# A two-layer Mamba, attention and expert kernel: one ring of PSUM banks for the B and C rows, the causal mask moved to VectorE, GpSimd's norm work placed behind the scans, and the output stage rearranged

## The reference, cut to what matters

```python
xn = layernorm(x)
# layer 0, branch s: Mamba, then an MLP
x_, z = split(xn @ in_proj.T);  x_ = silu(causal_conv(x_))
dt, Bm, Cm = split(x_ @ x_proj.T)            # 8, 16 and 16 numbers a row
dt = softplus(dt @ dt_proj.T + bias)
h[t] = exp(dt * A) * h[t-1] + dt * Bm[t] * x_[t]   # 256 channels x 16 states
y = (sum over states of h * Cm + x_ * D) * silu(z)
Z = rmsnorm(y @ out_proj.T + xn)
s = rmsnorm(gelu(Z @ w1.T + b1) @ w2.T + b2 + Z)
# layer 0, branch g: 4 groups, top 2 of 24 experts: product, layer norm, relu, product
g = layernorm(combine(experts(xn)) + xn)
x = x + s * silu(g);  xn = layernorm(x)
# layer 1, branch s: 8 heads of 128 over 8 sequences, 64 heads in all
sim = where(causal_mask, -max, q @ k.T);  s = softmax(sim) @ v @ w_out.T
# layer 1, branch g: top 2 of 128 experts, one product each
```

## Time and profile before

| what | before |
|---|---|
| median of 3 runs | 1617.62 us (1614.13 to 1619.54) |
| span of the profiled execution, first to last instruction | 1568.1 us |
| the profiled execution's own device time | not listed apart; the median lies 49.5 us above the span |
| busy share of the span: PE, DVE, ACT, POOL | 85%, 80%, 54%, 41% |
| chain of work that ended last: PE, DVE, ACT | 25%, 5%, 3% |
| mean granted clock of TensorE | 0.924 of full speed |

### The profile page before, as it was taken

One profiled execution on the slowest core, in us unless ns is written; L12 is line 12 of the kernel. 1 busy time (PEld: TensorE's weight loads), 2 busy tenths in 40 slices (PEclk: granted clock), 3 DMA queues, 4 the chain that ended last, 5 costly groups with the idle time before them and its releaser, 6 DMA issues. The chain is left out here.

```text
span 1568.1 us, 21870 instructions
## 1 busy us (share of the span) xinstructions
PE 1331.6 (85%) x7560; PEld 909.2 (58%) x7560; DVE 1253.2 (80%) x2263; ACT 848.2 (54%) x2090; POOL 650.5 (41%) x600
## 2 busy tenths in 40 slices
PE   7968788878987757899895696489999999999998
PEld 5534344443433336788784564356667677777776
DVE  6669989898889899999995857858988655567767
ACT  5367566565887765556551457553454444444452
POOL 0036554406798835545523755029600222146200
PEclk9979999888987958999997799699999999999999
DMA  6013455444343213545434210200010233112101
GB/s 215 0 29 106 128 142 143 122 117 135 106 135 121 94 59 105 144 128 139 130 95 154 56 35 2 98 15 1 1 39 17 55 84 102 40 33 47 22 15 41
DMA packets 75891, 127.31 MB, mean 81 GB/s; under 512 B 11758, under 2 KB 38606, under 8 KB 75174
## 3 DMA queue, kind: packets, MB, share of 16 engines
q1 hardware_dynamic: 56326, 75.04, 15.9%
q0 software_dynamic: 19456, 50.88, 12.2%
HBM read 85.51 MB, written 40.37 MB: 80 GB/s over the span
## 5 line engine op out<-in xcount | busy, mean ns | idle before, releaser
L643 DVE TENSOR_TENSOR_SCAN sc_st<-sc_dA,sc_st 128x1024 f32<-128x1024 f32 x128 | 293.2, 2331 | 0.0
L2070 DVE COPY at_pT<-at_p_t 128x512 f32<-128x512 f32 (+1 forms) x192 | 109.3, 599 | 132.4 <-PE at_p_t L1963 132.1
L2021 ACT ACTIVATE at_pr<-at_p_s,at_nmx 128x512 f32<-128x512 f32 (+3 forms) x256 | 131.3, 527 | 130.9 <-DVE at_nmx L2047 130.8
L1205 POOL DMA_INDIRECT g_state<-xn_scratch,moe_tab x96 | 116.1, 1209 | 183.6 <-POOLq L99 100.7
L613 DVE TENSOR_TENSOR sc_st<-sc_u,sc_p_b 128x1024 f32<-128x1024 f32 x128 | 154.9, 1210 | 45.2 <-PE sc_p_b L483 24.5
L422 ACT ACTIVATE sc_dA<-sc_dt,g_state 128x511 f32<-128x511 f32 x256 | 169.1, 710 | 16.2 <-DVE sc_st L643 12.7
L1942 PE MATMUL at_p_s<-att_xaT,at_qT 128*128 128x512 f32 (+3 forms) x512 | 172.0, 458 | 0.0
L1976 PEld LDWEIGHTS at_p_o<-at_V,at_pT 128*128 128x128 f32 x1280 | 152.4, 192 | 29.6 <-issue 28.8
L1236 POOL DMA_INDIRECT g_state<-r_scratch,moe_tab x96 | 114.2, 1189 | 113.8 <-PE e_bank L1335 79.7
L1976 PE MATMUL at_p_o<-at_V,at_pT 128*128 128x128 f32 x1280 | 153.7, 275 | 1.8 <-DVE g_state L2060 1.8
L621 DVE TENSOR_TENSOR sc_st<-sc_st,sc_p_c 128x1024 f32<-128x1024 f32 x128 | 155.1, 1212 | 0.0
(11 more groups left out here) (296 smaller groups left out, 2739.6 us busy)
## 6 DMA issues: line engine op xcount, KB each, us to landing
y_scratch<-g_state SPq DMA_DIRECT2D x24, 768.0 KB, 5.3
g_state<-W SPq DMA_DIRECT2D x48, 256.0 KB, 5.3
r_scratch<-g_state SPq DMA_DIRECT2D x16, 512.0 KB, 2.6
y_scratch<-g_state SPq DMA_DIRECT2D x24, 192.0 KB, 3.1
xn_scratch<-g_state SPq DMA_DIRECT2D x16, 256.0 KB, 4.5
g_state<-x SPq DMA_DIRECT2D x4, 512.0 KB, 6.0
g_state<-xn_scratch SPq DMA_DIRECT2D x8, 256.0 KB, 6.0
g_state<-x SPq DMA_DIRECT2D x1, 2048.0 KB
```

Source lines behind the costliest of these rows:

```text
L643: nc.vector.tensor_tensor_scan(st[:, m % RS, :, :].rearrange("p a b -> p (a b)"), dA[:, m % 4, :, :].rearrange("p a b -> p (a b)"), st[:, ...
L1205: nc.gpsimd.indirect_dma_start(out=self.xg[:, e % 4, h, :], out_offset=None, in_=self.xn_rows, in_offset=bass.IndirectOffsetOnAxis(ap=r.ta ...
L2021: ins = nc.scalar.activation(pr[:, n % 2, bank, c:c + K], p_s[:, bank, c:c + K], ACT.Exp, bias=nmx[:, n % 2, i:i + 1], accum_out=sums[:, n ...
L2070: v.tensor_copy(pT[:, n % 2, part, 0:cols], p_t[:, PT_BANK[part], 0:cols]).then_inc(pT_ready, 1)
```

## The change

**Scan stage.** `p_b` and `p_c` become one ring `p_bc` of three banks, with one pair of semaphores, `row_ready` and `row_used`. B row (i, j) has place 4i + 2j in it and C row (i, j) place 4i + 2j + 5; a row waits for the use of the row three places before it. `times_c` and `sum_states` now take one state of both halves where they took both states of one half. The B row (i+1, 1) is issued in step i, a step earlier than before. The extra turns of the expert program fall away in steps 22 to 42, and three are added at step 20 (two on TensorE, one on ScalarE and on VectorE). In the middle phase GpSimd's `weigh(u)` waits until the scans of step 25 + u have ended (or until a softplus half has ended, where one follows the scans).

**Output stage.** `out_T` is loaded alone first, then the rows of block 0, then `norm1`, `w1_T` and `b1`, rows 1 to 3, the other weights, the other rows; TensorE's first product waits for `out_T` alone. All eight projections come first, in two banks; the combining of the first four units follows the eighth. `e_yk` grows from 4 to 16 buffers, so that a gather waits for the combining of 16 tiles before and no longer of 4 before. The last two of eight weighings go to VectorE. `norm1` is copied into a PSUM bank, and the late scales read it there. The order on each engine is written out without `side_by_side`.

**Attention stage.** The mask products are gone. `M` is scaled by -SCALE, and VectorE does `tensor_tensor_reduce`: it adds a table `mask_wide` (128 x 512 float32, +1e30 above the diagonal) to the scores, writes the sum to `pr` in SBUF and accumulates the minimum in `nmx`. ScalarE's exponentials then run in place in `pr`. The bank is free once the maxima are done (`maxed` in place of `exped`). Scores and maxima run two heads ahead and queries three, with `pr` in 3 buffers and `sums` in 4; the first queries, scores and values are issued in another order.

```diff
+EVEN_FROM, EVEN_TO, FIRST_WINDOW = 22, 43, 26
+def uneven(i):
+    return not EVEN_FROM <= i < EVEN_TO
...
-        p_b = s.ps("p_b", [P, L])
-        p_c = s.ps("p_c", [P, 2, L])
+        p_bc = s.ps("p_bc", [P, 3, L])
...
+        def b_row(i, j):
+            return 4 * i + 2 * j
+        def c_row(i, j):
+            return 4 * i + 2 * j + 5
+        rows_in_order = sorted([b_row(i, j) for i in range(STEPS) for j in range(2)] +
+                               [c_row(i, j) for i in range(STEPS) for j in range(2)])
+        def rows_to(k):
+            return sum(1 for n in rows_in_order if n <= k)
...
-                if i % 4 == 3:
+                if i % 4 == 3 and uneven(i) or i == EVEN_FROM - 2:
...
+            def broadcast(k, b, n):
+                if rows_to(k - 3):
+                    pe.wait_ge(row_used, rows_to(k - 3))
+                nc.tensor.matmul(p_bc[:, k % 3, :], w["sel"][:, n * P:(n + 1) * P], bc3[:, b % 2, :], start=True,
+                                 stop=True).then_inc(row_ready, 1)
...
-                pe.wait_ge(hc_ready, 2 * i + h + 1)
-                for j in range(2):
+                pe.wait_ge(row_used, rows_to(c_row(i, j)))
...
-                broadcast_b(i, 1)
+                if i:
+                    broadcast_c(i - 1, 1)
...
-                broadcast_c(i)
+                broadcast_c(i, 0)
                 yield
                 if i:
                     sum_states(i - 1, 1)
+                if i + 1 < STEPS:
+                    broadcast_b(i + 1, 1)
                 yield
                 yield
-                if i % 2:
+                if i % 2 and uneven(i):
                     yield
+                if i == EVEN_FROM - 2:
+                    yield
+                    yield
+            broadcast_c(STEPS - 1, 1)
...
+            def times_c(i, j):
+                m = 2 * i % RS
+                k = c_row(i, j)
+                dve.wait_ge(row_ready, rows_to(k))
+                dve.wait_ge(scanned, 2 * i + 2)
+                states = st[:, m:m + 2, j, :]
+                nc.vector.tensor_tensor(states, states, p_bc[:, k % 3, :].unsqueeze(1).broadcast_to([P, HALF, L]),
+                                        ALU.mult).then_inc(row_used, 1)
...
+            pe.wait_ge(beside.out_in, 16)
+            for b in range(B):
+                project(b)
+                if b == B - 3:
+                    pe.wait_ge(beside.weights_in, 16 * len(beside.weights))
+                    beside.biases(pe, 0)
+                    beside.biases(pe, 1)
+            turn(0)
             hidden(0)
+            turn(1)
             for b in range(B):
                 if b + 1 < B:
                     hidden(b + 1)
...
+                if b + 2 < B:
+                    turn(b + 2)
+                mix(b)
+                if b + 2 < B:
+                    beside.biases(pe, b + 2)
...
+                if b == MIDDLE + 1:
+                    nc.scalar.activation(p_t[:, 0:D], w["norm1"], ACT.Copy).then_inc(norm_copied, 1)
+                    beside.centre(act, 0, 8)
...
+            def scale_chunk(c):
+                dve.wait_ge(root_ready, B + max(c, 1))
+                dve.wait_ge(norm_copied, 1)
+                t = slice(c * 8, (c + 1) * 8)
+                scale(s_rows[:, t, :], t, p_t[:, 0:D], s_ready)
...
+            for u in range(4):
+                beside.combine(dve, u)
...
+                if b + 2 < B:
+                    beside.combine(dve, 2 * b + 4)
+                    beside.combine(dve, 2 * b + 5)
+                if b == MIDDLE - 1:
+                    beside.scales(dve, 0)
+                if b == MIDDLE:
+                    scale_chunk(0)
...
+            scale_chunk(2)
+            beside.weigh_on_vector(dve, 6)
+            scale_chunk(3)
+            beside.weigh_on_vector(dve, 7)
+            dve.wait_ge(beside.x_in, 16)
+            for c in range(beside.CHUNKS):
+                beside.product(dve, c)
...
+        def wait_window(i):
+            b, q = divmod(i - 1, DS // 2)
+            if q in (3, 6):
+                pool.wait_ge(self.u_ready, 2 * (b + 1) + (q - 3) // 3 + 1)
+            else:
+                pool.wait_ge(self.scanned, 2 * i)
         def weigh(u):
             pool.wait_ge(self.centred, 2 * u + 2)
+            wait_window(FIRST_WINDOW + u)
...
+    YK = 16
...
+        sp.dma_start(*self.out_weight).then_inc(self.out_in, 16)
+        load_rows(0)
+        for dst, src in self.norm_weights:
+            sp.dma_start(dst, src).then_inc(self.norm_in, 16)
+        for b in range(1, 4):
+            load_rows(b)
         for dst, src in self.weights:
             sp.dma_start(dst, src).then_inc(self.weights_in, 16)
-        for b in range(B):
-            t = slice(b * TB, (b + 1) * TB)
-            sp.dma_start(self.xn_rows[:, t, :], self.xn_dram[:, t, :]).then_inc(self.xn_in[b], 16)
+        for b in range(4, B):
...
-        for q in range(2 * self.CHUNKS):
+        for q in range(2 * self.CHUNKS - 2):
...
+    def weigh_on_vector(self, dve, q):
+        v, w = self.nc.vector, self.w
+        o = self.o[:, 4 * q:4 * q + 4, :]
+        dve.wait_ge(self.centred, 4 * q + 4)
+        self.link(dve, v.tensor_tensor(o, o, w["ln_out_w"][:, :].unsqueeze(1).broadcast_to([P, 4, D]), ALU.mult))
+        v.tensor_tensor(o, o, w["ln_out_b"][:, :].unsqueeze(1).broadcast_to([P, 4, D]),
+                        ALU.add).then_inc(self.weighted_late, 1)
...
+                                         scale=-SCALE if n < 2 else 1.0).then_inc(fold_copied, 1)
...
-                        pe.wait_ge(exped, 3 * (n - 1) + k + 1)
+                        pe.wait_ge(maxed, 3 * (n - 1) + k + 1)
                     for i in tiles:
                         bank, c = SIM_AT[i]
                         K = (i + 1) * P
-                        nc.tensor.matmul(p_s[:, bank, c:c + K], qT[:, n % 3, i * P:(i + 1) * P], xaT[:, b, 0:K],
-                                         start=True, stop=False)
-                        ins = nc.tensor.matmul(p_s[:, bank, c + i * P:c + K], w["ident_bf"], w["mask_bf"],
-                                               start=False, stop=True)
+                        ins = nc.tensor.matmul(p_s[:, bank, c:c + K], qT[:, n % 3, i * P:(i + 1) * P], xaT[:, b, 0:K],
+                                               start=True, stop=True)
...
+            for n in range(3):
+                query(n)
+            score(0)
+            for k in range(4):
                 value(k)
-            query(0)
-            query(1)
-            score(0)
+            score(1)
+            for k in range(4, NH):
...
-                if n + 1 < NI:
-                    score(n + 1)
+                if n + 2 < NI:
+                    score(n + 2)
...
-                    act.wait_ge(turned, 3 * (n - 1))
-                if n >= 3:
-                    act.wait_ge(out_used, n - 2)
+                if n >= 4:
+                    act.wait_ge(out_used, n - 3)
...
+                        row = pr[:, n % 3, bank, c:c + K]
+                        ins = nc.scalar.activation(row, row, ACT.Exp, scale=-1.0, bias=nmx[:, n % 2, i:i + 1],
+                                                   accum_out=sums[:, n % 4, i:i + 1])
...
-                        ins = v.tensor_reduce(nmx[:, n % 2, i:i + 1], p_s[:, bank, c:c + (i + 1) * P], AX_X, ALU.max,
-                                              negate=True)
+                        K = (i + 1) * P
+                        ins = v.tensor_tensor_reduce(out=pr[:, n % 3, bank, c:c + K], in0=p_s[:, bank, c:c + K],
+                                                     in1=w["mask_wide"][:, L - K:L], scale=1.0,
+                                                     scalar=float(np.finfo(np.float32).max), op0=ALU.add, op1=ALU.min,
+                                                     accum_out=nmx[:, n % 2, i:i + 1])
...
-        "ident_bf": np.eye(P, dtype=np.float32).astype(bf16),
-        "mask_bf": (np.triu(np.ones((P, P), np.float32), 1) * np.float32(-1e30)).astype(bf16),
+        "mask_wide": c(np.concatenate([np.zeros((P, 3 * P), np.float32),
+                                       np.triu(np.ones((P, P), np.float32), 1) * np.float32(1e30)], axis=1)),
```

501 lines of the change are left out of this document (237 added, 264 removed).

## The result

The changed kernel takes 1563.99 us (median of 4 runs, 1562.68 to 1565.59) where the kernel before takes 1617.59: 53.6 us less, a ratio of 0.966 with a 95% interval of 0.964 to 0.968. It is faster, as forecast, but by little more than half of the 92 us summed up, and the time lies outside the range.

A forecast was written before the change was run, and what follows sets the result against it. VectorE was taken to bound the scan phases, TensorE attention, and no engine the output stage. 1568.1 - 31 - 28 - 33 = 1476; with 49.5, 1526 us, range 1505 to 1560.

The forecast's parts named there:

- the median lies 49.5 us above the span, which I keep: Whole kernel: the gap between the 1568.1 us span and the measured median, added unchanged to the forecast time.
- three signs that the prediction named for being wrong: Reduction above 4.2 us a head; third scan phase longer; middle phase still waiting over 13 us for the sum of states.
- -31: Scan stage: middle phase -21, first phase -8, third phase -6, end +4 us; bounds -10 and -67.
- -28: Output stage: 118 us against 146, with late scales giving 6.6 of it; bounds -14 and -36.
- -33: Attention stage: masks 21.5, heads 0 to 8 4, the rest of TensorE's idle time 7.5 us; upper bound -42.
- +4 of the end: Scan stage's end: last expert product now behind the final turning, costing 4 us, between 1.6 and 9.4.
- 16 x 0.7 = 11 us stay lost: Middle scan phase: 16 GpSimd units at 12.0 us against 11.3 a step keep 11 us lost, leaving 21 gained.
- First phase: Scan stage: 8 of 13.5 idle VectorE us gained in the first phase, 6 of 18.1 in the third.
- 21.5 + 7.5 = 29: Attention: 21.5 us from dropping masks on 55 heads, plus 7.5, half of TensorE's remaining 14.3 idle us.
- GpSimd's pace: Rival, scan stage: the new wait holds the gathers, the middle phase gains nothing, 1549 us; chance 0.14.
- limit attention: Rival: VectorE's mask replacement costs its upper bound, attention gains 15 instead of 33 us, 1544 us; chance 0.10.
- Gathers not held by scans: Rival, middle scan phase: a GpSimd unit takes 10.4 us, the 11 us left go too, 1515 us; chance 0.06.

The follow-up runs named there:

- experiment 2: Changed kernel with 4 buffers for the output stage's gathered rows instead of 16, on the result's chip: 1545.28 us, 0.955 of the kernel before.
- experiment 5: Changed kernel with 4 output-stage buffers and attention's layer 1 gathers spread four to a head, on another chip: 1485.50 us, 0.947 of the kernel before.
- experiment 9: The changed kernel, unedited, on another chip, where the kernel before takes 1573.1 us: 1472.00 us, ratio 0.937.
- experiment 18: Changed kernel with four bf16 products of 128 columns a head put back into the score groups: 1497.31 us, 0.955 of the kernel before.

## Why the prediction was wrong, point by point

**The step that failed** is "the median lies 49.5 us above the span, which I keep". It took those microseconds for something around the program that no edit touches. They lay inside it: 1.8 us are around the span, and the rest is late signals in the output and attention stages, in executions other than the one on the page. The change made them more: 52.3 us became 91.8 where they occur (46 and 92 by medians). So the chip of the result gives 1472 + 92 = 1564 where the sum had 1476 + 49.5. On the chips without late signals the sum gives 1476 + 1.8 = 1478 us, and the kernel takes 1472 to 1475. None of the three signs that the prediction named for being wrong came: each looked at the work, and none at the 49.5 us.

That the 16 buffers made the output stage's share grow from 20.9 to 53.9 us is shown by experiment 2: four buffers bring the stage from 187.4 to 167.5 us, and the rest of 167.5 over the 146.2 of the same buffers elsewhere (experiment 5), 21.3, is what the kernel before loses too. The prediction had let the combining, 16 buffers deep, hide behind TensorE, which holds on the other chips only. Why attention's share grew from 31.4 to 37.9 no run tells, and what holds the signals stays open.

**The sum by stage,** against experiment 9, from the page's execution of before: scan stage up to the start of the output stage -39.7 for -31, output stage -26.0 for -28, attention -32.0 for -33, and -0.7 in between; together -98.4 for -92.

**Scan stage.** From first to last scan it is -44.1; the first scan starts 1.4 us later, and from last scan to the output stage's start the time grows from 11.1 to 14.1, +3.0 for the +4 of the end. The middle phase, from the scans of step 22 to those of step 42, goes from 265.9 to 234.4 us: -31.5, where 21 was forecast. The mis-sized term is "16 x 0.7 = 11 us stay lost": VectorE's idle time falls from 23.9 to 9.3 us, 14.6 for the 15.3 forecast, but its busy time falls from 242.0 to 225.1, 16.9 for 5.2. Little stayed lost: a scan takes 2.30 us for the undisturbed 2.225, and the softplus lines their 0.69. First phase -3.3 for 8, third -9.3 for 6.

**Output stage,** forecast 118 us from its start: 923.3 - 803.9 = 119.4 in experiment 9, from 145.4 before.

**Attention stage,** -32.0 of which experiment 18 gives the mask products 22.4. Heads 0 to 8 give 6.6 us (78.13 to 71.57) where 4 was taken, the other 55 heads 25.4 where 21.5 + 7.5 = 29 was. The masking reduction costs 112.0/64 + 4 x 0.08 = 2.1 us a head with its read-outs, within the bounds 1.7 and 4.2, and plain heads take 7.20 us with TensorE busy throughout.

**The rivals.** GpSimd's pace did not hold the middle phase. VectorE did not limit attention as a whole, but it does decide heads 6 to 8, where experts run beside: it is busy 9.25, 8.97 and 9.42 us of their 9.49, 9.28 and 9.60 in experiment 9, TensorE 8.2 to 8.3, and head 7 takes longer than before (8.96). Gathers not held by scans: they are held. In the trace of before, the 29 gathers L1215 that overlap a scan take 1.83 us on average (up to 2.79), the 24 beside L613 or L621, which read one operand from PSUM, 0.95. None of the rivals was what happened; the one that was missing is that an execution's time and its trace must be the same execution's.

## What to carry to other kernels

Before summing against a median, make the trace's own span agree with it; a gap of 3% is work or waiting that this trace doesn't show, and it can react to the edit. Where a helper engine is told by a fixed table when to work, the table and the number of turns of the other engines are one change: the wait without the even turns cost 112 us here, the even turns without the wait 9. And a deeper buffer lets a helper run longer without a pause: on one chip that cost the output stage 20 us, on the others it gained 13, so a buffer's depth is worth timing on more than one chip. Whether pacing the gathers pays where signals are late, these runs don't show.

## What the runs showed of the hardware

Chips can differ by more than runs: the same kernel before takes 1572 us on three chips and 1619 on another, and the changed kernel 1472 to 1475 and 1564. Where signals of TensorE came late, the waits were up to 28.15 us long. The two long ones shown ended 5 and 3 us after GpSimd's last gather in a row, others while gathers still went out (8.66 us, up to 819.07). Twelve gathers in a row in the scan stage of the same execution held no signal. What makes a chip do so stays open, and so does whether other GpSimd work than gathers would.

A gather's issue takes 0.95 us beside VectorE operations that read PSUM and 1.83 on average beside scans. The combined mask and minimum (L2127) runs at the rate of a plain addition, 0.69 us for 512 columns, and its read-out takes 0.08 us.
